# A routed expert's down product: the second half of its contraction as a stacked tail, and its transposes moved ahead of it

## The reference

```
g = silu(x @ w_gate[e].T) * (x @ w_up[e].T)      # 176 channels
y = g @ w_down[e].T                              # contraction over 176
out = sum over the two experts of cw * y, plus a shared expert of hidden size 352
```

## Time and profile before

| | us |
|---|---|
| median of the runs | 720.18 |
| the profiled execution | 717.36 |
| its span, first to last instruction | 715.4 |
| TensorE matmuls busy | 616.5 (86%) |
| TensorE weight loads busy | 511.4 (71%) |
| VectorE busy | 489.7 (68%) |
| ScalarE busy | 349.4 (49%) |
| GpSimd busy | 309.8 (43%) |
| token stage, up to the last matmul (L89) | 0 to 226 |
| experts' loop, first to last up product | 235.6 to 404.6 |
| attention stage, from the first gather | from 410 |

### The profile page before, as it was taken

How to read it: one execution, slowest core, us unless ns; L and a number is a source line. 1 busy time by engine, 2 the same in 40 slices (tenths; PEclk the granted TensorE clock), 3 DMA queues, 4 the chain that set the end, 5 groups by cost and what they waited for, 6 DMA issues and landing times. The chain is left out here.

```text
span 715.4 us, 23762 instructions
## 1 busy us (share of the span) xinstructions
PE 616.5 (86%) x8674; PEld 511.4 (71%) x8674; DVE 489.7 (68%) x1317; ACT 349.4 (49%) x870; POOL 309.8 (43%) x401
## 2 busy tenths in 40 slices
PE   1988979979966799999999768888888888988885
PEld 1777868868855699999999756666666666656663
DVE  3565556645683356666666548888888887988886
ACT  4438538547434234444444334555555555555442
POOL 1064083171270820000000033777777776777775
PEclk9999999999988689999999958999999999999997
DMA  8044445345245733333343360222522252323120
GB/s 292 33 140 175 162 148 217 113 170 217 69 169 204 259 104 118 112 121 117 111 124 118 106 227 10 63 92 65 190 88 92 61 212 62 92 62 91 33 62 30
DMA packets 59726, 88.20 MB, mean 123 GB/s; under 512 B 8236, under 2 KB 46348, under 8 KB 58604
## 3 DMA queue, kind: packets, MB, share of 16 engines
q1 hardware_dynamic: 50700, 69.43, 28.8%
q0 software_dynamic: 6656, 16.86, 6.8%
q10 hardware_dynamic: 2272, 0.53, 0.3%
HBM read 46.54 MB, written 40.24 MB: 121 GB/s over the span
## 5 line engine op out<-in xcount | busy, mean ns | idle before, releaser
L1628 POOL TENSOR_TENSOR tick_a<-lane 128x1 f32<-128x1 f32 x32 | 6.3, 196 | 155.4 <-POOLq L826 153.1
L1631 POOL DMA_INDIRECT yg<-d_grouped_y,from_row x64 | 63.3, 990 | 15.5 <-issue 11.6
L87 PE MATMUL e_up<-wb,xb 128*128 x144 | 53.8, 373 | 0.7 <-issue 0.7
L1479 ACT ACTIVATE hid<-a_ring,b 64x128 f32<-64x128 f32 x32 | 11.6, 363 | 87.3 <-remote 50.8
L973 ACT ACTIVATE hb<-e_h 88x256 fp32r<-88x256 f32 x72 | 27.4, 380 | 54.3 <-PE e_h L948 54.3
L1462 ACT ACTIVATE with_mem<-a_ring 128x340 f32<-128x340 f32 x128 | 47.1, 447 | 12.2 <-PE a_ring L1320 12.2
L87 PE MATMUL e_y<-wd,hb 88*128 x146 | 49.3, 338 | 1.6 <-DVE hb L1012 1.6
L1005 DVE TENSOR_TENSOR h_sb<-e_up,silu 128x176 f32<-128x176 f32 x72 | 24.6, 341 | 36.5 <-ACT silu L968 36.5
L813 POOL TENSOR_TENSOR ticks<-lane 128x1 f32<-128x1 f32 x4 | 2.2, 562 | 106.3 <-DVE slot_i L731 106.3
L88 PE MATMUL e_up<-wb,xb 128*128 x144 | 47.5, 330 | 0.0
L89 PE MATMUL e_up<-wb,xb 128*128 x144 | 47.5, 330 | 0.0
(11 more groups left out here) (281 smaller groups left out, 2051.2 us busy)
## 6 DMA issues: line engine op xcount, KB each, us to landing
xg<-d_rows SPq DMA_DIRECT2D x77, 128.0 KB, 2.0
d_grouped_y<-y_sb SPq DMA_DIRECT2D x73, 128.0 KB, 1.8
d_v<-v_half SPq DMA_DIRECT2D x8, 544.0 KB
v<-d_v SPq DMA_DIRECT2D x4, 1088.0 KB, 8.8
d_q<-halves SPq DMA_DIRECT2D x8, 512.0 KB
d_k<-halves SPq DMA_DIRECT2D x8, 512.0 KB
skT<-d_k SPq DMA_DIRECT2D x8, 512.0 KB
total<-d_base SPq DMA_DIRECT2D x8, 512.0 KB
```

Source lines behind the costliest of these rows:

```text
L87: pe.matmul(out, a[0], b[0], start=start, stop=False)
L1631: pool.indirect_dma_start(yg[tile % GATHERS][:, k, :], None, d["grouped_y"], bass.IndirectOffsetOnAxis(ap=c["from"][:, k, tile:tile + 1], ...
```

## The change

The hidden channels are split as 128 and 48 (`FT`), no longer as 88 and 88. The transposes of h cover 128 columns each. In the second one, the 48 tail channels stand twice: at partitions 0 to 47 and, 64 further on (`FD`), at 64 to 111; what lies between is zero. After the high part is made, VectorE subtracts it in place in partitions 64 to 111, so the tail tile holds high channels below and low channels above; the high down weights are loaded twice to match. The down product is then three matmuls over the 128 channels, one over the stacked tail (112 partitions, high and low at once) and one over 48 partitions for high by low weights: five, and not six. VectorE makes h in two instructions, the second one writing both copies of the tail, and the low part in two. On TensorE the h transposes now stand right behind the x transposes, and `down` is last in the slot. The load of the down weights becomes four transfers, since head and tail channels go to different partitions; the semaphore count that ScalarE waits for follows. Sizes of the tiles and of what is zeroed ahead of the loop follow as well.

```diff
--- before.py
+++ after.py
@@ -43,6 +43,8 @@
 E, F, FS = 8, 176, 352
 TOP = 2
 FC = F // 2
+FT = F - P
+FD = P // 2
 G1 = H // 4
 EPS = 1e-6
 LN_EPS = 1e-5
@@ -127,7 +129,7 @@
         silu = sb("silu", [P, KC, ST])
         v_half = sb("v_half", [P, TS, NH, HE])
         halves = c["halves"]
-        stage_w, stage_d = c["mem_rows"][:, 0:W_PIECE], c["mem_rows"][0:FC, 0:D_PIECE]
+        stage_w, stage_d = c["mem_rows"][:, 0:W_PIECE], c["mem_rows"][:, 0:D_PIECE]
         n_sg, n_su, n_sd = KC * (FS + E), KC * FS, len(SF) * H
         shared_w = sb("shared_w", [P, 2 * (n_sg + n_su + n_sd)], F32R)
 
@@ -243,6 +245,15 @@
                 sp.wait_ge(s_base, b * 2 * NS + 2 * (s + 1))
                 sp.dma_start(base_d[b * NS + s, :, :, :], x_in[b % 2][:, half(s), :]).then_inc(s_bst[s], 16)
 
+            def stage_down(b):
+                to = stage_d.rearrange("p (e f n) -> p e f n", f=2, n=H)
+                source = d["wd_all"][:, b * D_PIECE:(b + 1) * D_PIECE].rearrange("p (e f n) -> p e f n", f=2, n=H)
+                head = P - FC
+                sp.dma_start(to[0:FC, :, 0, :], source[:, :, 0, :]).then_inc(s_std, 16)
+                sp.dma_start(to[FC:P, :, 0, :], source[0:head, :, 1, :]).then_inc(s_std, 16)
+                sp.dma_start(to[0:FT, :, 1, :], source[head:FC, :, 1, :]).then_inc(s_std, 16)
+                sp.dma_start(to[FD:FD + FT, :, 1, :], source[head:FC, :, 1, :]).then_inc(s_std, 16)
+
             def store_half(b, s, what):
                 slot, _ = half_slot(b, s, what)
                 sp.wait_ge(s_sum, b * NQ + 4 * s + (4 if what == "k" else 2))
@@ -269,7 +280,7 @@
                     tokens(b + 1, [s_x[(b + 1) % 2]] * 2)
                 store_values(b, 0)
                 sp.wait_ge(s_wl, 2 * b + 1)
-                sp.dma_start(stage_d, d["wd_all"][:, b * D_PIECE:(b + 1) * D_PIECE]).then_inc(s_std, 16)
+                stage_down(b)
                 store_values(b, 1)
                 if b == B - 1:
                     tails()
@@ -532,7 +543,7 @@
                 high(b, 3)
                 values_out(b, 1, 1)
                 silu_of(b, 4)
-                act.wait_ge(s_std, 16 * (b + 1))
+                act.wait_ge(s_std, 64 * (b + 1))
                 act.activation(w["wd"][0][:, b * D_PIECE:(b + 1) * D_PIECE], stage_d, ACT.Copy).then_inc(s_wh, 1)
                 if b + 1 < B:
                     normed(b + 1, 0)
@@ -828,8 +839,9 @@
         xg = [sb(f"xg{i}", [P, H]) for i in range(UNROLL)]
         xb = [[sb(f"xb{q}{i}", [P, KC, P], F32R) for i in range(2)] for q in range(2)]
         silu = [sb(f"silu2{q}", [P, F]) for q in range(2)]
-        h_sb = [sb(f"h_sb{q}", [P, F]) for q in range(2)]
-        hb = [[sb(f"hb{q}{i}", [FC, 2, P], F32R) for i in range(2)] for q in range(2)]
+        h_sb = [sb(f"h_sb{q}", [P, 2 * P]) for q in range(2)]
+        hb = [sb(f"hb{q}", [P, 2, P], F32R) for q in range(2)]
+        hb_low = [sb(f"hb_low{q}", [P, P], F32R) for q in range(2)]
         y_sb = [sb(f"y_sb{q}", [P, H]) for q in range(2)]
 
         ps_x = [bank(f"e_x{q}") for q in range(2)]
@@ -909,10 +921,13 @@
 
                 pe.wait_ge(s_hl, n - 1)
                 pe.wait_ge(s_y, n - 3)
-                for f in range(2):
-                    cols = bass.ds(at_dn + f * H, H)
-                    mm = three(pe, ps_y[q][:, 0:H], [hb[q][i][:, f, :] for i in range(2)],
-                               [w["wd"][i][:, cols] for i in range(2)], f == 0, f == 1)
+                cols, tail = bass.ds(at_dn, H), bass.ds(at_dn + H, H)
+                three(pe, ps_y[q][:, 0:H], [hb[q][:, 0, :], hb_low[q][:, :]],
+                      [w["wd"][i][:, cols] for i in range(2)], True, False)
+                pe.matmul(ps_y[q][:, 0:H], hb[q][0:FD + FT, 1, :], w["wd"][0][0:FD + FT, tail],
+                          start=False, stop=False)
+                mm = pe.matmul(ps_y[q][:, 0:H], hb[q][0:FT, 1, :], w["wd"][1][0:FT, tail],
+                               start=False, stop=True)
                 mm.then_inc(s_dn, 1)
 
             def word_of(group):
@@ -941,13 +956,13 @@
 
                 pe.wait_ge(s_ga[(u + 2) % UNROLL], 16 * (slot // UNROLL) + (16 if u < 2 else 32))
                 transposed((u + 2) % UNROLL, q)
-                down(at_dn, n, q)
 
                 pe.wait_ge(s_h, n)
                 for f in range(2):
-                    mm = pe.transpose(ps_h[o][0:FC, f * P:(f + 1) * P], h_sb[o][:, f * FC:(f + 1) * FC],
+                    mm = pe.transpose(ps_h[o][:, f * P:(f + 1) * P], h_sb[o][:, f * P:(f + 1) * P],
                                       c["ident"][:, :])
                 mm.then_inc(s_hT, 1)
+                down(at_dn, n, q)
             down(at[0][1], SLOTS + 4, 0)
 
         @block.scalar
@@ -970,7 +985,7 @@
                     high_tokens(q)
                     act.wait_ge(s_hT, n)
                     act.wait_ge(s_dn, n - 2)
-                    act.activation(hb[o][0][:, :, :], ps_h[o][0:FC, 0:2 * P].rearrange("p (k n) -> p k n", k=2),
+                    act.activation(hb[o][:, :, :], ps_h[o][:, 0:2 * P].rearrange("p (k n) -> p k n", k=2),
                                    ACT.Copy).then_inc(s_hh, 1)
 
             with act.Fori(0, SLOTS // UNROLL) as it:
@@ -982,9 +997,9 @@
 
             for q in range(2):
                 link(dve.memset(h_sb[q][:, :], 0.0))
-            for i in range(2):
-                ins = (dve.tensor_scalar(hb[0][i][:, :, :], c["ident"][0:FC, :].unsqueeze(1).broadcast_to([FC, 2, P]),
-                                       0.0, None, ALU.mult))
+            dve.tensor_scalar(hb[0][:, :, :], c["ident"][:, :].unsqueeze(1).broadcast_to([P, 2, P]),
+                              0.0, None, ALU.mult)
+            ins = dve.tensor_scalar(hb_low[0][:, :], c["ident"][:, :], 0.0, None, ALU.mult)
             ins.then_inc(s_init, 1)
             for j in range(2):
                 dve.wait_ge(s_xh, 5 + j)
@@ -1002,15 +1017,20 @@
                     q, o = u % 2, (u - 1) % 2
                     dve.wait_ge(s_silu, n + 1)
                     dve.wait_ge(s_hT, n - 1)
-                    dve.tensor_tensor(h_sb[q][:, :], ps_up[q][:, F:2 * F], silu[q][:, :],
+                    dve.tensor_tensor(h_sb[q][:, 0:P], ps_up[q][:, F:F + P], silu[q][:, 0:P], ALU.mult)
+                    dve.tensor_tensor(h_sb[q][:, P:2 * P].rearrange("p (i n) -> p i n", i=2)[:, :, 0:FT],
+                                      ps_up[q][:, F + P:2 * F].unsqueeze(1).broadcast_to([P, 2, FT]),
+                                      silu[q][:, P:F].unsqueeze(1).broadcast_to([P, 2, FT]),
                                       ALU.mult).then_inc(s_h, 1)
                     dve.wait_ge(s_xh, n + 3)
                     dve.tensor_tensor(xb[q][1][:, :, :], ps_x[q][:, 0:H].rearrange("p (k n) -> p k n", k=KC),
                                       xb[q][0][:, :, :].bitcast(F32), ALU.subtract).then_inc(s_xl, 1)
                     result(n, q, it * 32 + 16 + (16 if u >= 2 else 0))
                     dve.wait_ge(s_hh, n)
-                    dve.tensor_tensor(hb[o][1][:, :, :], ps_h[o][0:FC, 0:2 * P].rearrange("p (k n) -> p k n", k=2),
-                                      hb[o][0][:, :, :].bitcast(F32), ALU.subtract).then_inc(s_hl, 1)
+                    dve.tensor_tensor(hb_low[o][:, :], ps_h[o][:, 0:P], hb[o][:, 0, :].bitcast(F32), ALU.subtract)
+                    low = hb[o][FD:FD + FT, 1, :]
+                    dve.tensor_tensor(low, ps_h[o][FD:FD + FT, P:2 * P], low.bitcast(F32),
+                                      ALU.subtract).then_inc(s_hl, 1)
             result(SLOTS + 4, 0, SLOTS * 8 + 16)
 
             dve.wait_ge(s_tables, 1)
@@ -1708,7 +1728,7 @@
             c["start"], c["pack"] = sb("start_i", [P, NI], I32), sb("pack_i", [P, NI // UNROLL], I32)
             w["wqkv"] = [sb(f"wqkv{i}", [P, WQKV], F32R) for i in range(2)]
             w["wb"] = [sb(f"wb{i}", [P, WUP], F32R) for i in range(2)]
-            w["wd"] = [sb(f"wd{i}", [FC, E * 2 * H], F32R) for i in range(2)]
+            w["wd"] = [sb(f"wd{i}", [P, E * 2 * H], F32R) for i in range(2)]
             tokens_phase(nc, d, c, w)
             experts_phase(nc, d, c, w)
         attention_phase(nc, d, c, w)
```

## The result

The kernel after takes 733.54 us (median of 4 runs, 729.63 to 738.25) beside 719.39 us for the kernel before (4 runs): ratio 1.0204 [1.0168, 1.0240], 14.15 us slower. The forecast was 729.2 us, 722.0 to 733.5. The direction and the mechanism in the loop hold; the time lies 4.3 us above the forecast, 0.04 us past the upper end. Three of the four runs of before are those on record ahead of the prediction, so this pair doesn't stand fully side by side. Repeated on two other occasions, side by side, the pair gave 1.0184 and 1.0169.

A forecast was written before the change was run, and what follows sets the result against it. TensorE's stream was taken to bound the experts' loop. The profiled 717.36 us + 8.5 (66 slots) + 0.5 (wd load) made 726.4; on the runs' median, 2.8 above that execution, 729.2 us, range 722 to 733.5.

The forecast's parts named there:

- (4): Experts' loop, fifth down matmul over 48 rows: leaving and re-entering the full array costs 0.385 us a slot.
- The first two rivals: Fifth down matmul: a plain step, 703.8 us (8%); or its charge partly hidden, 0.19 to 0.34 a slot (11%).
- the third: Experts' loop: VectorE's six instructions become the bound, slot 2.15 us, total 714; decides only together with the first rival; 2%.
- (1): Experts' loop, down product: five matmuls instead of six save one step, -0.12 us a slot.
- (2): Experts' loop: h transposes ahead of down remove the 0.13 us wait for VectorE's low part; slot 2.12 from 2.256.
- (3): Experts' loop: VectorE's six instructions hold it 1.5 us a slot, and h transposes load 128 columns; no cost.
- the first rival: Experts' loop: the 48-row matmul is a plain step, slot 2.00 us, kernel 703.8 us; 8%.
- (5): Load of wd as four transfers: costs nothing in three batches, +0.5 us in the last.

The follow-up runs named there:

- Experiment 1: Kernel after with its fifth down matmul over 112 rows instead of 48: 702.19 us beside 710.35 for before, ratio 0.9890.
- 7: Kernel after with its fifth down matmul over 65 rows instead of 48: 707.98 us beside 707.65 for before, slot 2.096.
- 5: Kernel after with its 48-row matmul issued twice in a row: 729.96 us beside 707.65 for before, slot 2.527.
- experiment 3: Kernel before with only the order changed, down behind the h transposes: 702.77 us, ratio 0.9898 to before.
- 4: Kernel before with only the down weights' load changed, four transfers instead of one: 709.82 us, ratio 1.0001 to before.

## Why the prediction was right or wrong

**What bounds the kernel, and (4), the change of shape: right.** The slot is set by TensorE's stream, and going from the full array to 48 rows and back costs what the 8-row transposes of the token stage cost. From the stacked tail over L929 and L89 to L90 it takes 0.210 + 0.311 + 0.266 = 0.787 in the mean, where plain steps are 0.12 + 0.12 + 0.16 = 0.40: 0.387, forecast 0.385. Experiment 1 takes the charge away, 7 does so with the smallest possible edit, and 5 shows that it is paid once for each change. The first two rivals fall with them, and the third, since VectorE holds no slot of the kernel after. That the total of the charge comes out to 0.002 is in part luck: the parts named in (4) add up to 0.36 to 0.38, and the three distances foretold, 0.21, 0.32 and 0.27, to 0.40.

**(1), (2), (3): right for the kernel after.** The slot is 2.376, forecast 2.385; experiment 3 measures (2) alone at 2.125, forecast 2.12. The loop's +7.97 is 0.5 under the forecast's +8.5. One term in (2) was mis-sized: the second low part was put 0.21 behind the first, and stands 0.30 behind it. In the slot of 2.376 this is covered; without the charge it would have been the next thing late, and the first rival's 703.8 us, worked out at 2.00 a slot, would have come out about 6.7 higher (experiment 1's 2.101 a slot, 66 times), not all of it from this term.

**(5): the size was right, and small.** The copy of wd started some 0.7 later for the four loads (all executions taken together), forecast +0.5. It started at 200.92, outside the 196.2 to 199.5 foretold: 195.50 + 5.42, of which 2.44 is the later issue, that is, a token stage that was already late ahead of it.

**What failed is the last step, the total.** "717.36 + 8.5 + 0.5" sets everything outside the loop and the wd load to exactly the one execution shown, and the range took its width from the bounds of (4) and (5) alone. Neither allowed for two executions of the same code that differ, though the median of the runs shown was already 2.8 us above the profiled one. The runs show how large that is. TensorE's granted clock is 0.5 in some stretches (1.2 GHz in place of 2.4) and full in the others, so a run's half-clock time is 2 x (1 - mean clock) x span. Over 115 runs in groups of one kernel on one occasion, an added us of it goes with 0.28 us (± 0.02) of run time. The runs of after had more of it than those of before beside them, 86.1 against 80.8 us on one chip and 84.2 against 77.9 on another, with an uncertainty of 2 to 3 us on each difference: worth some 1.6 us, and 86.7 in the first four runs. At equal half-clock time the pairs differ by 11.3 ± 0.8 and 9.9 ± 0.9 us, where 8.0 of the loop and 0.7 of the loads make 8.7.

So the 14.15 us are: 8.0 the loop, 0.7 the loads, about 1.6 more half-clock time, 1.2 to 2.6 in stages around the loop that no run ties to a part of the change, and the rest, some 2 us, put down to the scatter of four runs and to runs that weren't all side by side, since the pair repeated gave 12.5 and 12.1. Only the 8.0 is shown by experiments; the split of the rest is an estimate. Whether the change causes the added half-clock time is open: experiments 1, 3 and 4 have 83.9, 85.4 and 84.1 us of it beside the same 80.8, each more than before by one to two times the uncertainty of the difference, so they neither tie it to one part nor rule one out, and it may be chance.

**The range.** Had the spread of executions been one of its terms, as wide on either side as the 2.8 us between the profiled execution and the median shown, its upper end would have been some 736 us.

## What to carry to other kernels

Read a TensorE stream by the distance from start to start, and count a matmul over 64 rows or fewer between wide ones as three steps of 256 columns more than it looks: 65 rows or more, the added ones over a harmless term, cost a plain step. Before work is split finer, look at what order the queues are in: one moved call gained as much as the finished split, and the copy ahead of the low parts was the next thing to move. A forecast that is built on one execution needs a term for how far two executions of the same stages lie apart.

## What the runs showed that was not expected

The border of the charge is sharp: 64 rows 2.377 us a slot, 65 rows 2.096. A VectorE instruction at partition 64 between two at partition 0 loses the overlap on both sides, 0.10 to 0.11 us each (0.08 of overlap and 0.01 to 0.03 of gap). A slot can lose more than the lateness of its release: in experiment 1 the first down weights were late in 24 of 66 slots by a mean of 0.04 us over all slots, while the slot lay 0.10 over the plain sum; why is open. And the attention stage, whose code is the same in all kernels, took 293.9 to 302.1 us in four executions on one chip, a spread as large as what the loop lost.
